# Layer-norm statistics on ScalarE, and units of the scan taken in pairs

## What is computed

```python
def _layernorm(x, g, b):
    m = mean(x, -1); v = mean((x - m) ** 2, -1)
    return (x - m) * rsqrt(v + 1e-5) * g + b

# state-space layers: 512 inner channels d, 16 states n, 512 steps t
xz = norm(x) @ in_proj;  x_in, z = split(xz)
u = silu(conv4(x_in) + conv_b)
dt_r, B, C = split(u @ x_proj)          # 64, 16, 16
dt = softplus(dt_r @ dt_proj + dt_b)
h[d, n] = h[d, n] * exp(dt[d] * A[d, n]) + dt[d] * u[d] * B[n]     # for each t
y[d] = sum_n h[d, n] * C[n] + u[d] * D[d]
x = x + gate * ((y * silu(z)) @ out_proj)

# attention layers, each with two layer norms
q, k, v = norm(x) @ Wq, Wk, Wv; y = softmax(q) @ (softmax(k).T @ v)
x = x + silu(norm(y) * (1 + scale) + shift) @ W_out
```

## Time and profile before

| what | value |
|---|---|
| median of 3 runs | 2321.26 us (2316.08 to 2328.55) |
| the profiled execution | 2319.99 us; its span 2318.2 us |
| VectorE busy | 1996.4 us (86%) |
| TensorE busy | 1937.2 us (84%) |
| GpSimd busy | 1922.5 us (83%) |
| ScalarE busy | 1754.9 us (76%) |
| mean granted TensorE clock | 0.921 of full |

### The profile page before, as it was taken

One profiled execution on the slowest core, in us unless ns is written; L12 is line 12 of the kernel. 1 busy time (PEld: TensorE's weight loads), 2 busy tenths in 40 slices (PEclk: granted clock), 3 DMA queues, 4 the chain that ended last, 5 costly groups with the idle time before them and its releaser, 6 DMA issues. The chain is left out here.

```text
span 2318.2 us, 23856 instructions
## 1 busy us (share of the span) xinstructions
PE 1937.2 (84%) x5712; PEld 994.6 (43%) x5712; DVE 1996.4 (86%) x2730; ACT 1754.9 (76%) x2737; POOL 1922.5 (83%) x1610
## 2 busy tenths in 40 slices
PE   5867778898888889889888978889897978777886
PEld 4433334435344444435444443534444443323353
DVE  4368898989989899999989999998989989898862
ACT  2467869698887869787887978778897977768643
POOL 0068998989898998998889898998999898999950
PEclk9787899999999989999999989999999988898898
DMA  5046565655455565655555565564656556665620
GB/s 229 1 135 167 153 188 143 188 152 158 148 163 158 162 189 150 168 165 145 152 152 173 161 176 156 164 177 133 173 160 173 147 169 172 166 183 156 185 83 18
DMA packets 170554, 358.84 MB, mean 155 GB/s; under 512 B 19544, under 2 KB 27952, under 8 KB 161712
## 3 DMA queue, kind: packets, MB, share of 16 engines
q1 hardware_dynamic: 150726, 274.07, 37.0%
q0 software_dynamic: 9216, 67.11, 15.2%
q10 hardware_dynamic: 10474, 16.14, 1.9%
HBM read 284.85 MB, written 5.29 MB: 125 GB/s over the span
## 5 line engine op out<-in xcount | busy, mean ns | idle before, releaser
L659 POOL TENSOR_TENSOR state<-state,c_rows 128x512 f32<-128x512 f32 x1024 | 1315.9, 1352 | 139.6 <-DVE state L1142 71.6
L1445 PE MATMUL bank<-state,const_sb 128*128 128x512 f32 x1536 | 769.8, 619 | 67.5 <-POOL state L659 58.8
L1142 DVE TENSOR_TENSOR_SCAN state<-decay,bank 128x512 f32<-128x512 f32 x640 | 764.3, 1206 | 28.1 <-ACT decay L891 26.2
L883 ACT ACTIVATE bank<-b_rows 128x512 f32<-128x512 f32 x640 | 380.1, 594 | 251.7 <-DVE state L1139 164.6
L1132 DVE TENSOR_TENSOR bank<-kept,bank 128x512 f32<-128x512 f32 x640 | 436.0, 681 | 103.3 <-ACT bank L883 101.5
L650 POOL TENSOR_TENSOR state<-kept,b_rows 128x512 f32<-128x512 f32 x384 | 513.0, 1336 | 0.1
L1139 DVE TENSOR_TENSOR_SCAN state<-bank,state 128x512 f32<-128x512 f32 x384 | 466.4, 1215 | 3.4 <-POOL state L650 3.3
L891 ACT ACTIVATE decay<-kept,ssm_pack 128x512 f32<-128x512 f32 x640 | 455.8, 712 | 2.7 <-ACT x_dbl L830 1.5
L1445 PEld LDWEIGHTS bank<-state,const_sb 128*128 128x128 f32 x1536 | 286.1, 196 | 383.4 <-issue 212.2
L875 ACT ACTIVATE bank<-kept,ssm_pack 128x512 f32<-128x512 f32 x384 | 261.2, 680 | 79.0 <-DVE state L1142 68.2
L1343 PE MATMUL bank<-kept,ssm_pack 128*128 128x512 f32 x512 | 257.3, 636 | 33.8 <-DVE kept L1092 17.2
(11 more groups left out here) (136 smaller groups left out, 2018.5 us busy)
## 6 DMA issues: line engine op xcount, KB each, us to landing
b_rows<-flat_rows SPq DMA_DIRECT2D x512, 256.0 KB, 3.5
c_rows<-flat_rows SPq DMA_DIRECT2D x512, 256.0 KB, 3.3
state<-state POOLq DMA_DIRECT2D x64, 1024.0 KB, 8.3
out<-x_res ACTq DMA_DIRECT2D x8, 512.0 KB, 3.2
x_next<-x ACTq DMA_DIRECT2D x6, 512.0 KB, 4.4
ssm_pack<-ssm_pack ACTq DMA_DIRECT2D x1, 2035.0 KB, 19.5
ssm_pack<-ssm_pack SPq DMA_DIRECT2D x1, 2035.0 KB, 10.0
state<-ada_w ACTq DMA_DIRECT2D x1, 1536.0 KB, 10.5
```

The costliest lines, as they stand in the source:

```text
L659: pool.tensor_tensor(st, st, c_rows[:, row % ROWS], ALU.mult).then_inc(m_prod, 1)
L883: act.activation(mix_banks[g % BANKS][:], b_rows[:, row % ROWS], ACT.Copy).then_inc(m_brow, 1)
L1142: ins = dve.tensor_tensor_scan(st, decay[:, nth(g) % DECAYS], mixed, 0.0, ALU.mult, ALU.add)
L1445: pe.matmul(y_banks[c2][:], ident, state[:, g % STATES], start=False, stop=(g == in_bank[-1])).then_inc(m_sum, 1)
```

## The change

The statistics of all 48 norms move to ScalarE: per tile one pass `Copy` with an accumulated output (the sum), one small operation that makes minus the mean of the 4 tiles, per tile one pass `Square` with the mean as bias and an accumulated output, and one small operation that adds eps. The passes' full outputs go to a tile that is overwritten later. GpSimd's `root` stays.

The kinds of units go by pairs of neighbours (6 BESIDE and 10 SPREAD pairs in 16, the same shares). GpSimd's injection and its product with C take a pair as one operation of 128x1024, the row broadcast. For a SPREAD pair ScalarE copies the row once, into the bank freed longest ago, and VectorE multiplies both units' dt*u by it as one operation over two neighbouring banks, the row's and another one. `bank_plan` picks the banks by when they are freed; where the neighbour is free only after the scan directly ahead of the pair, the product stands directly before the pair's first scan, otherwise one scan earlier.

The loads of `ada_w`, the gate rows and the second pack move from ScalarE's queue at the start to SyncE's, behind the mask row. The leads and lags and all stage tables are set anew (`DECAY_LEAD` 2 to 3, `SUM_LAG` 4 to 5, `FOLDED_LAG` 12 to 14); in the new tables the stage `norm` of attention kind B and of `before` of kind 0 has 0 ticks, `ynorm` of kind B has 1, `norm` and `ynorm` of kinds A, C and D have 2 to 12 (before, with the work on VectorE, all of these had 0 to 3). The tables, the counting of semaphores by pairs and the waits of `moments` on its sources in `before` are left out of the diff.

```diff
-BANK_LEAD, DECAY_LEAD, WEIGHT_LAG, SUM_LAG = 2, 2, 2, 4
+BANK_LEAD, DECAY_LEAD, WEIGHT_LAG, SUM_LAG = 2, 3, 2, 5
-FOLDED_LAG = 12
+FOLDED_LAG = 14
-KINDS = ((BESIDE, SPREAD) * 3 + (SPREAD, SPREAD)) * 2
-TAIL_UNITS, POST_END, PREP_END = 3, {1: 24, 2: 26}, 60
-SETUP_UNITS, FIRST_PREP, FIRST_ATT = (-139, -68), (-81, -18), (-70, 34)
-ATT_UNITS = ((32, 92), (93, 154), (154, 218), (218, 281))
+KINDS = (BESIDE, SPREAD, SPREAD, BESIDE, SPREAD) * 2 + (BESIDE, SPREAD, SPREAD, BESIDE, SPREAD, SPREAD)
+TAIL_UNITS, POST_END, PREP_END = 4, {1: 24, 2: 26}, 60
+SETUP_UNITS, FIRST_PREP, FIRST_ATT = (-146, -67), (-82, -7), (-63, 33)
+ATT_UNITS = ((31, 91), (93, 155), (155, 218), (218, 286))
...
+def bank_plan():
+
+    freed, of_unit, of_row, scanned, lead = {0: -3, 1: -1, 2: -2}, {}, {}, {}, {}
+    for p in range(ALL_UNITS // HC):
+        first, second, third = sorted(freed, key=freed.get)
+        if pair_kind(p) == SPREAD:
+            of_row[p], scanned["row", p] = first, freed[first]
+            soon = abs(second - first) == 1
+            first, second = second if soon else third, first
+            lead[p] = int(soon)
+        for g, k in ((p * HC, first), (p * HC + 1, second)):
+            of_unit[g], scanned[g] = k, freed[k]
+            freed[k] = g
+    return of_unit, of_row, scanned, lead
+
+
+BANK_OF, ROW_BANK, BANK_FREED, PRODUCT_LEAD = bank_plan()
...
+        mix = ctx.enter_context(nc.psum_tensor("mix_banks", [P, BANKS, 512], F32))
+        mix_banks = [mix[:, k, :] for k in range(BANKS)]
+        single = [ctx.enter_context(nc.psum_tensor(f"bank{k}", [P, 512], F32)) for k in range(5)]
+        bank = single[0:HC] + mix_banks + single[HC:]
+        y_banks, att_banks, pb = bank[0:HC], [bank[5], bank[2], bank[3]], bank[6:8]
...
             sp.dma_start(ssm_sb[1][:], ssm_packs[1]).then_inc(s_ssm_w[1], 16)
+            sp.dma_start(ada_sb[1], ada_w[1].rearrange("(k p) n -> p k n", p=P)).then_inc(s_cond_w[1], 16)
             sp.dma_start(x_next[1][:], rows_by_tile(x[1])).then_inc(s_x[1], 16)
             sp.dma_start(order_i, order.partition_broadcast(P)).then_inc(s_order, 16)
+            sp.dma_start(ada_sb[2], ada_w[2].rearrange("(k p) n -> p k n", p=P)).then_inc(s_cond_w[2], 16)
             sp.dma_start(film_sb[3], film_w[3].rearrange("(k p) n -> p k n", p=P)).then_inc(s_cond_w[3], 16)
+            for n in range(2):
+                sp.dma_start(gate_bias[:, n], gate_rows[n].partition_broadcast(B)).then_inc(s_gate_rows, 16)
+            sp.dma_start(ssm_sb[2][:], ssm_packs[2]).then_inc(s_ssm_w[2], 16)
             sp.dma_start(att_sb[3][:], att_packs[3]).then_inc(s_att_w[3], 16)
...
-                pool.tensor_tensor(state[:, g % STATES], dtu[:, c], b_rows[:, row % ROWS], ALU.mult).then_inc(m_inject[BESIDE], 1)
+                for k in range(g, g + HC):
+                    state_free(pool, k - STATES)
+                pool.tensor_tensor(pair_states(g), dtu[:, c:c + HC], by_pair(b_rows[:, row % ROWS]),
+                                   ALU.mult).then_inc(m_inject[BESIDE], 1)
 
             def weight(g):
                 si, half, n, c2, c = split(g)
                 row = half * N + n
-                if c2 == 0:
-                    pool.wait_ge(c_loaded[row % ROWS], 16 * (si * (HALVES * N // ROWS) + row // ROWS + 1))
-                pool.wait_ge(m_scan, g + 1)
-                st = state[:, g % STATES]
-                pool.tensor_tensor(st, st, c_rows[:, row % ROWS], ALU.mult).then_inc(m_prod, 1)
+                pool.wait_ge(c_loaded[row % ROWS], 16 * (si * (HALVES * N // ROWS) + row // ROWS + 1))
+                pool.wait_ge(m_scan, g + HC)
+                st = pair_states(g)
+                pool.tensor_tensor(st, st, by_pair(c_rows[:, row % ROWS]), ALU.mult).then_inc(m_prod, 1)
...
-                if part == 0 and is_unit(g - WEIGHT_LAG):
-                    weight(g - WEIGHT_LAG)
+                last = g - WEIGHT_LAG
+                if part == 0 and is_unit(last) and last % HC == HC - 1:
+                    weight(last + 1 - HC)
                 if part == 0:
                     return
-                if is_unit(g + INJECT_LEAD) and kind_of(g + INJECT_LEAD) == BESIDE:
-                    inject(g + INJECT_LEAD)
+                first = g + INJECT_LEAD
+                if is_unit(first) and first % HC == 0 and kind_of(first) == BESIDE:
+                    inject(first)
                 for n, (source, into) in enumerate(FOLDS):
                     done = g - FOLD_LAG + 1
...
-            for n in range(2):
-                act.dma_start(gate_bias[:, n], gate_rows[n].partition_broadcast(B)).then_inc(s_gate_rows, 16)
-            for layer in SSM:
-                act.dma_start(ada_sb[layer], ada_w[layer].rearrange("(k p) n -> p k n", p=P)).then_inc(s_cond_w[layer], 16)
-            act.dma_start(ssm_sb[2][:], ssm_packs[2]).then_inc(s_ssm_w[2], 16)
...
+            def moments(norm, src, scratch, link, done, k):
+
+                sums, minus, squares, var_eps = (norm[n][:, :, 0] for n in ("sum", "minus", "squares", "var_eps"))
+                for t in range(TT):
+                    ins = act.activation(scratch[:, t, :], src[:, t, :], ACT.Copy, accum_out=sums[:, t:t + 1])
+                    if t == TT - 1:
+                        ins.then_inc(link, 1)
+                    yield
+                act.wait_ge(link, k * NORM_LINKS + 1)
+                act.activation(minus, sums, ACT.Copy, scale=-1.0 / D).then_inc(link, 1)
+                act.wait_ge(link, k * NORM_LINKS + 2)
+                for t in range(TT):
+                    ins = act.activation(scratch[:, t, :], src[:, t, :], ACT.Square, bias=minus[:, t:t + 1],
+                                         accum_out=squares[:, t:t + 1])
+                    if t == TT - 1:
+                        ins.then_inc(link, 1)
+                    yield
+                act.wait_ge(link, k * NORM_LINKS + 3)
+                act.activation(var_eps, squares, ACT.Identity, scale=1.0 / D, bias=norm["eps"][:, 0, 0:1]).then_inc(done, 1)
 
...
+                yield from w.to("norm")
+                if layer == 0:
+                    act.wait_ge(s_x[s], 8 * (b - s) + 16)
+                else:
+                    taken(act, post_fill(scan_index(2, b), "gather0"))
+                    taken(act, post_fill(scan_index(2, b), "gather1"))
+                if ai == 0:
+                    act.wait_ge(s_x_other, 16)
+                    act.wait_ge(s_eps, 2)
+                yield from w.over(stages["norm"], 2 * TT, moments(att_norm, src, xn, a_links, a_var, 2 * ai))
...
+                yield from w.to("ynorm")
+                att_taken(act, ai, "y0", "y1")
+                yield from w.over(stages["ynorm"], 2 * TT, moments(att_norm, y, xn, a_links, a_var, 2 * ai + 1))
...
-            def moments(norm, src, var, link):
-
-                stats, mv = norm["stats"], norm["mv"]
-                for t in range(TT):
-                    ins = dve.bn_stats(stats[:, t, :], src[:, t, :])
-                link(ins)
-                for t in range(TT):
-                    ins = dve.bn_aggr(mv[:, t, 0:2], stats[:, t, :])
-                link(ins)
-                dve.tensor_reduce(norm["var_eps"][:, :, 0], mv[:, :, 1:3], AX, ALU.add)
-                dve.tensor_reduce(norm["minus"][:, :, 0], mv[:, :, 0:1], AX, ALU.max, negate=True).then_inc(var, 1)
-
...
-                dve.wait_ge(m_brow, nth(g))
-                row = mix_banks[g % BANKS]
-                dve.tensor_tensor(row[:], dtu[:, c, :], row[:], ALU.mult).then_inc(m_inject[SPREAD], 1)
+                past(dve, m_scan, BANK_FREED[g] + 1)
+                dve.wait_ge(m_brow, nth_pair(g // HC))
+                at, row = BANK_OF[g], ROW_BANK[g // HC]
+                both = mix[:, at:row + 1, :] if row > at else mix[:, at:(row - 1 if row else None):-1, :]
+                dve.tensor_tensor(both, dtu[:, c:c + HC, :], by_pair(mix_banks[row]), ALU.mult).then_inc(m_inject[SPREAD], 1)
 
             def scan(g):
-                st, mixed = state[:, g % STATES], mix_banks[g % BANKS][:]
+                st, mixed = state[:, g % STATES], mix_banks[BANK_OF[g]]
                 dve.wait_ge(m_decay[kind_of(g)], nth(g))
-                dve.wait_ge(m_inject[kind_of(g)], nth(g))
+                dve.wait_ge(m_inject[kind_of(g)], nth_pair(g // HC))
                 if kind_of(g) == BESIDE:
                     ins = dve.tensor_tensor_scan(st, mixed, st, 0.0, ALU.mult, ALU.add)
                 else:
...
-                    if is_unit(g + 1) and kind_of(g + 1) == SPREAD:
-                        inject(g + 1)
+                    for first in (g, g + 1):
+                        if is_unit(first) and first % HC == 0 and kind_of(first) == SPREAD and PRODUCT_LEAD[first // HC] == first - g:
+                            inject(first)
```

118 lines of the change are left out of this document (61 added, 57 removed), and 34 rows, old and new, of tables (ATT_STAGES, POST_STAGES, PREP_STAGES).

## The result

The changed kernel takes 2268.12 us, median of 4 runs (2262.8 to 2272.73); the kernel before, run beside it, takes 2321.53 (2316.08 to 2328.55). The ratio is 0.9772, 95% interval 0.9748 to 0.9796: 53 us less. The forecast was 2264.

The account below looks back on a forecast made before the run. VectorE was taken to set the pace, in a close loop with ScalarE. Middle: 2095 - 82 (norms) - 22 (products) + 61 (dependences) - 113 + 93 (waits) = 2032; with +7 for the close 2264 us, range 2185 to 2340.

Parts of the forecast that it names:

- The opening: Before the first scan: an earlier mask row gains some 5 us, two norms cost 2.3 each; put at 0, bounds -8 and +8.
- A norm on ScalarE: Eight passes and two small operations take 4.3 us per norm, 41 x 4.3 = 176 us in the middle.
- rival (c): On ScalarE `Square` is not in the tables in use; two loads per norm, 105 us more; 2317 to 2369; chance 0.05.
- About 100 us less: Sign that the forecast is right: VectorE's busy time in the middle falls by about this much.
- A dependence: On VectorE, an instruction needing its direct predecessor's result costs 0.12 us more; 512 of them cost 61 us.
- Rival (e): Dependences between neighbours on VectorE are free, so without the 61 us the time is 2203 us; chance 0.05.
- The 0.50 chance: The chance given to the forecast itself, a sum over VectorE's issued work and its waits for ScalarE, 2264 us.
- The waits for ScalarE: VectorE's waits for B rows and decays in the middle go from 113 to 113 - 70 + 50 = 93 us.
- The 70: Saving in VectorE's waits for B rows, as two scans instead of one lie between freed bank and product; bounds 0 and 87.
- Rival (a): ScalarE's bursts lead: the wider window saves nothing, half the norms' time stalls VectorE; 2372 us; chance 0.11.
- Rival (d): The gains cancel: 61 us of dependences stay and 40 of the 70 do not come; 2304 us; chance 0.12.
- GpSimd's pairs: Joined operations on GpSimd save 0.2 to 0.3 us each, 140 to 220 in all, but buy nothing directly, only cover.

Follow-up runs that it names:

- dve_norms: The changed kernel with only the norms' statistics moved back to VectorE, at the same places of the same tables: 2288.38 us, ratio 0.9868 to the kernel before.
- loads_back: The changed kernel with the five large loads back on ScalarE's queue at the start: 2275.69 us, ratio 0.9785 to the kernel before.
- act_norms: The kernel before with only the norms' statistics moved to ScalarE, its tables and unpaired operations kept: 2441.72 us, ratio 1.0519.
- dep_before: The kernel before with each VectorE product made to wait for the scan ahead of it, which the data don't need: 2351.07 us, ratio 1.0133.
- short_passes: The changed kernel with each norm's passes on ScalarE reading 32 of the 256 columns: 2253.37 us, ratio 0.9717 to the kernel before.

## Why the prediction was right, point by point

**The total and its stretches** were right: 2264 against 2268, and -63 in the middle against -58.6, +7 in the close against +7.3 (5.5 of it the norms, by `dve_norms`). The opening was put at 0 and gave 4.4; the reason named for a gain, the mask row, is the right one by `loads_back` (6.3), and the norms that were to eat it cost 1.7 by `dve_norms`, not 4.6.

**What the operations cost** was right in the main. A norm on ScalarE takes 4.41 us (4.3 taken), without table loads, so rival (c) is out, and ScalarE is busy for 1686 us (about 1690). The norms were taken as 82 us of VectorE; `act_norms` and `dve_norms` put them at 68 and 73 of its busy time. VectorE's busy time was to fall by 82 + 22 less the 0.09 of lost overlap at each of 512 dependences, 46: 58; it fell by 62. "About 100 us less", as the text had it, forgot that lengths which overlap count once, so that a lost overlap adds to the busy time. The wide product has a length of 1.23, against the 1.19 of the earlier trace rows, and takes 1.14 from start to start instead of 1.11: 378 - 320 x 1.14 = 13 us were saved by joining, not 22.

**A dependence** was 0.12 us behind a scan, as taken. Behind the wide product it is 0.18, so the term is 320 x 0.12 + 192 x 0.18 = 73 (79 with 0.14), not 61; by the 235 and 162 that stand without a wait it is 57. Rival (e) is out. But `dep_before` shows that of 56 added us only 31 reach the time, and no term of the sum had such a share. The 0.50 chance was on a sum in which each microsecond on VectorE is one of the span. `dve_norms` pays 28 of 73 in the middle, `dep_before` 31 of 56.

**The waits for ScalarE** were put at 93 and came to 85: without the norms they fall from 113 to 53 (`dve_norms`), 60 and not 70, and the norms add 32 and not 50. (Some of the 32 is time that the norms, when VectorE does them, give ScalarE.) The two errors offset each other in part, which is luck. The 70 were put down to the window and to the wait at the product. The waits for rows and decays do rise by 56 us when the window is narrowed (85 to 141), but the time rises by 117 (81 without the norms), since the copy blocks ScalarE and what is queued behind it. As for the norms, `short_passes` takes only 5 us off the middle for 59 us less of ScalarE, and strewing 32 of them is worth 16. Rival (a), ScalarE's bursts lead, is false for this arrangement and is just what happens in the old one: `act_norms` is 122 us slower, with 215.6 + 49.6 = 265 us of waits for rows and decays. With the narrow window the move gains nothing in the middle and loses 15 in all. Rival (d), the gains cancel, did not come either; its own 2304 lies 17 us under the kernel before, more than the 12 us that the text counts as little change.

**GpSimd's pairs** were the plain miss. "This buys nothing directly; it is cover" failed: taking them apart loses 41 of the 53 us. The saving per pair was taken too large as well: 0.2 to 0.3 us by the mean lengths, 140 to 220 in all, where the busy time gives 98 over 704 pairs and the distances from start to start 0.15 each. So GpSimd was busy for 1811 us, not for 1685 to 1765. The error was to price GpSimd by lengths, against the prediction's own rule, and to read from 3.3 us of waits that an engine at 91% has room in a kernel that becomes shorter. The cover for `root` held for the most part: GpSimd waits 40.5 + 16.0 us for the sums, and VectorE 13.5 for injections (5.7 in `dve_norms`), far from the 40 to 80 us named for the case that the cover went.

**The tables** were a part of the change that the prediction did not price at all, except through how far the norms are strewn. With the old ones the changed kernel is 5.6% slower than before. That no term stood for them was the largest gap; the sum came out since with the new tables VectorE is idle for as long as it was with the old operations and the old tables (177 and 174 us). That was not argued, and is luck as far as the prediction goes.

The single differences do not add up to the whole: 41 (pairs) + 22 (norms) + 2 to 8 (loads) is more than 53, and the window's 117 and the tables' 185 stand beside them. Each is what one part is worth with all others in place. The total was right because the busy time of VectorE was, and the idle time stayed equal; the prediction's account of the idle time names the window and the norms, and leaves out GpSimd's time and the tables, which were worth 41 and 185 us.

## What to carry to other kernels

Where four engines feed one another in a laid-out order, price the operations from start to start, and then don't count them at full worth: 31 of 56 and 28 of 73 us were paid here, and work taken from the engine that follows close behind (GpSimd, 91% busy) was worth 41 us. A change of operations and the order laid out for them belong together: the same operations ran in 0.977 or in 1.056 of the time before, and moving the norms took 22 us off in the changed kernel and put 122 on in the kernel before. Before a wait is priced by its row, ask what is queued behind the one who waits: the row copy's later start showed as 42 us at its reader and cost 117.
